# Attention columns through TensorE and ten of 24 counts through ScalarE, in the first stage of a GAT + SAGE kernel

## The reference

```python
h = relu(layernorm(x))
xp = (h @ W).reshape(N, 4, 256)                    # GAT, H = 4 heads of C = 256
a_src = einsum('nhc,hc->nh', xp, att_src);  a_dst = einsum('nhc,hc->nh', xp, att_dst)
e = leaky_relu(a_src[src] + a_dst[dst], 0.2)       # edges and self loops
alpha = softmax of e over the edges of each destination
x = x + relu(segment_sum(xp[src] * alpha, dst).reshape(N, D) + bias)
h = relu(layernorm(x))                             # then two SAGE layers
x = x + sage(relu(sage(h, W_self0, W_neigh0, b0)), W_self1, W_neigh1, b1)
```

## Time and profile before

| | us |
|---|---|
| median of 3 runs (3427.87 to 3436.28) | 3431.57 |
| profiled execution | 3438.69 |
| its span | 3437.0 |
| end of prepare's last operation (DVE L484), from the span's start | 97.77 |

### The profile page before, as it was taken

One profiled execution on the slowest core, in us unless ns is written; L12 is line 12 of the kernel. 1 busy time (PEld: TensorE's weight loads), 2 busy tenths in 40 slices (PEclk: granted clock), 3 DMA queues, 4 the chain that ended last, 5 costly groups with the idle time before them and its releaser, 6 DMA issues. The chain is left out here.

```text
span 3437.0 us, 66696 instructions
## 1 busy us (share of the span) xinstructions
PE 2969.7 (86%) x20462; PEld 1710.6 (50%) x20462; DVE 2364.8 (69%) x3944; ACT 1205.7 (35%) x2639; POOL 1637.3 (48%) x1592
## 2 busy tenths in 40 slices
PE   0558888579999997899799999998699999997998
PEld 0335554368888886444344444444344444443444
DVE  8657898599999998788566666665455555554433
ACT  3653344268888886444112222222000000001111
POOL 5002232357777775232366666663466666662000
PEclk9989998889999999899899999999899999999999
DMA  2558997369888888777699999996899999996454
GB/s 79 163 174 297 317 366 262 119 227 323 311 310 298 308 316 271 245 218 226 220 359 339 329 341 329 327 338 228 308 342 324 332 318 338 315 327 242 135 140 119
DMA packets 282530, 934.91 MB, mean 272 GB/s; under 512 B 53795, under 2 KB 54799, under 8 KB 282368
## 3 DMA queue, kind: packets, MB, share of 16 engines
q0 software_dynamic: 217792, 713.64, 59.4%
q1 hardware_dynamic: 64576, 219.26, 20.4%
HBM read 879.78 MB, written 130.57 MB: 294 GB/s over the span
## 5 line engine op out<-in xcount | busy, mean ns | idle before, releaser
L1517 PE MATMUL gagg_sum_ps<-gagg_got,gagg_hot_hi 128*128 128x256 f16 x3520 | 591.6, 273 | 94.7 <-ACT gagg_hot_hi L1488 33.0
L1405 POOL DMA_INDIRECT gagg_got<-xs_rows,all_idx x440 | 505.8, 1150 | 191.8 <-issue 132.3
L1488 ACT ACTIVATE gagg_hot_hi<-gagg_hot,all_mem 128x128 f16<-128x128 f16 x1760 | 538.0, 388 | 167.5 <-DVE gagg_hot L1428 167.5
L1405 POOL DMA_INDIRECT agg_got<-h_rows,all_idx x440 | 435.3, 989 | 320.4 <-PE agg_sum_ps L1533 182.1
L1833 POOL DMA_INDIRECT agg_got<-h_rows,all_idx x440 | 437.2, 994 | 268.1 <-PE agg_sum_ps L1986 144.5
L1453 DVE TENSOR_TENSOR sums_acc<-agg_sum_ps,sums_acc 125x1024 f32 x220 | 269.5, 1225 | 324.3 <-PE agg_sum_ps L1533 320.6
L1517 PE MATMUL gagg_sum_ps<-gagg_got,gagg_hot_lo 128*128 128x256 f16 x1760 | 481.4, 273 | 0.0
L1898 DVE TENSOR_TENSOR sums_acc<-agg_sum_ps,sums_acc 125x1024 f32 x220 | 268.8, 1222 | 247.6 <-PE agg_sum_ps L1986 245.9
L1986 PE MATMUL agg_sum_ps<-agg_got,all_mem 128*128 128x512 f16 x1760 | 414.3, 383 | 25.1 <-DVE all_mem L1867 16.7
L1533 PE MATMUL agg_sum_ps<-agg_got,agg_hot 128*128 128x512 f16 x1760 | 417.6, 380 | 20.3 <-DMA agg_got<-h_rows,all_idx 16.1
L1517 PEld LDWEIGHTS gagg_sum_ps<-gagg_got,gagg_hot_hi 128*128 128x128 f16 x3520 | 329.3, 98 | 138.3 <-ACT gagg_hot_hi L1488 70.6
(11 more groups left out here) (290 smaller groups left out, 3995.8 us busy)
## 6 DMA issues: line engine op xcount, KB each, us to landing
edg_piece<-slot_rows POOLq DMA_DIRECT2D x56, 512.0 KB
edg_w_buf<-in_L_gnn_W_self_dram SPq DMA_DIRECT2D x32, 512.0 KB, 7.8
edg_w_buf<-in_L_gnn_W_neigh_dram SPq DMA_DIRECT2D x32, 512.0 KB, 10.1
split_w<-edg_w_out SPq DMA_DIRECT2D x32, 512.0 KB, 8.9
agg_got<-h_rows,all_idx POOLq DMA_INDIRECT x880, 7.2
x_rows<-fin_val POOLq DMA_DIRECT2D x25, 500.0 KB
h_rows<-fin_h POOLq DMA_DIRECT2D x25, 500.0 KB
out_dram<-neigh_rows POOLq DMA_DIRECT2D x25, 500.0 KB
```

The lines of the kernel that those rows point to most:

```text
L1405: g.indirect_dma_start(out=got[:, k % R, :], out_offset=None, in_=rows_in[:, :], in_offset=bass.IndirectOffsetOnAxis(ap=idx[:, k:k + 1], a ...
L1488: last = a.activation(hot_hi[:, u % HOTS, h, :], hot[:, u % HOTS, :], ACT.Copy, scale=high_e[:, ds(s, 1), h])
L1517: t.matmul(sum_ps[n % 2][:, h * C:(h + 1) * C], hot_k[:, u % HOTS, h, :], got[:, u % R, part * D + h * C:part * D + (h + 1) * C], start=(u ...
```

## The change

All edits are in prepare.

- ACT makes ten of the 24 counts (borders 1 to 10) as the sum of sign(dst - t*125 + 0.5) over the row of 512 edges. POOL makes the ten offsets `lines` at the start. DVE makes the other fourteen and turns ACT's sums into counts with one small operation.
- att is loaded as 16 rows of 128 (no broadcast), and TensorE turns it into `att_c`, 128 x 16.
- For every strip k TensorE turns W's eight 128 x 128 blocks (`turn_w`, two PSUM banks of four blocks), ACT copies each bank to SBUF (`w_c`), and TensorE multiplies each block with the two att columns that belong to it (`weigh`), float32, adding up two blocks for a head in PSUM.
- POOL's weigh and ACT's gather are gone, and so is DVE's own strip (L468 to L475).
- DVE copies `w_att` out of PSUM after its four rows, then takes largest(1), then copies idx, rel and src_tile, and makes the low parts of W after these; before, the low parts came first.
- TensorE's list now holds the eight turn_w and eight weigh between the tile transposes and the transposes of the gathered rows.

```diff
-    for t in range(1, NT):
+    for t in range(BY_SIGN + 1, NT):                       # vector; BY_SIGN = 10
         last = v.tensor_scalar(junk[:, :, :], dst_f[:, :, :], float(t * TN), 0.0,
                                ALU.is_lt, ALU.add, accum_out=below[:, t - 1:t])
-        if t < NT - 1:
-            step(last)
-    last.then_inc(counted, 1)
+        step(last)
+    v.wait_ge(signed, BY_SIGN)
+    v.tensor_scalar(below[:, 0:BY_SIGN], signs[:, :], -0.5, 0.5 * CPP * CH, ALU.mult, ALU.add).then_inc(counted, 1)
...
     row(3)
+    v.wait_ge(w_att_done, KT)
+    for q in range(2):
+        last = v.tensor_copy(w_att[:, :, q * H:(q + 1) * H], w_att_ps[:, :, :, q])
+    step(last)
+    largest(1, w_att[:, :, :].rearrange("p k n -> p (k n)"))
+    v.wait_ge(turned, 1)
+    (the three copies of L478)
     for k in range(KT):
         v.wait_ge(hi_done, k + 1)
         v.scalar_tensor_tensor(w16[:, k, D:2 * D], ...)
-    (the eight products of L471, the three copies of L478)
-    v.wait_ge(tmp_used, 2 * OWN)
-    largest(1, w_att[:, :, :].rearrange("p k n -> p (k n)"))
     scale(1)
```

```diff
 @block.gpsimd
+    step(g.iota(lines[:, :], [[-TN, BY_SIGN]], base=-TN, channel_multiplier=0, ...))
+    g.tensor_scalar(lines[:, :], lines[:, :], 0.5, None, ALU.add).then_inc(lines_ready, 1)
     g.wait_ge(padded, 1)
...
-    g.dma_start(att_sb[:, q, :], att.rearrange("h c -> (h c)").partition_broadcast(P)).then_inc(att_loaded, 16)
+    g.dma_start(att_rows[q * KT:(q + 1) * KT, :], att.rearrange("h (j c) -> (h j) c", c=P)).then_inc(att_loaded, 16)
...
-    weigh(0) ... weigh(6)
```

```diff
 @block.scalar
+    a.wait_ge(lines_ready, 1)
+    a.wait_ge(dst_loaded, 32)
+    a.wait_ge(dst_tail, 16 * TAILS)
+    for t in range(BY_SIGN):
+        a.activation(junk_a[:, t], edges[:, :, 1, :], ACT.Sign, bias=lines[:, t:t + 1],
+                     accum_out=signs[:, t:t + 1]).then_inc(signed, 1)
+    a.wait_ge(att_turned, 1)
+    a.activation(att_c[:, :], att_c_ps, ACT.Copy).then_inc(att_moved, 1)
+    for n in range(KT * KT // PER_BANK):                   # 16 moves of 128 x 512
+        k, half = divmod(n, KT // PER_BANK)
+        a.wait_ge(w_turned, n + 1)
+        if k >= 2:
+            a.wait_ge(w_att_done, k - 1)
+        a.activation(w_c[:, k % 2, half * PER_BANK:(half + 1) * PER_BANK, :], w_c_ps[n % 2][:, :, :], ACT.Copy).then_inc(w_moved, 1)
     a.wait_ge(up_ready, 1)
     (the eight high parts of L366)
-    for k in range(2, OWN):
-        gather(k)
```

```diff
 @block.tensor
+    def turn_w(k):
+        for half in range(KT // PER_BANK):
+            n = k * (KT // PER_BANK) + half
+            if n >= 2:
+                t.wait_ge(w_moved, n - 1)
+            for c in range(PER_BANK):
+                j = half * PER_BANK + c
+                last = t.transpose(w_c_ps[n % 2][:, c, :], w_sb[:, k, j * P:(j + 1) * P], ident[:, :])
+            last.then_inc(w_turned, 1)
+    def weigh(k):
+        t.wait_ge(w_moved, (k + 1) * (KT // PER_BANK))
+        for j in range(KT):
+            h, first = divmod(j, KT // H)
+            last = t.matmul(w_att_ps[:, k, h, :], w_c[:, k % 2, j, :], att_of[:, j, :],
+                            start=(first == 0), stop=(first == KT // H - 1))
+        last.then_inc(w_att_done, 1)
+    t.wait_ge(made, 1)
+    t.wait_ge(att_loaded, 32)
+    t.transpose(att_c_ps, att_rows[:, :], ident[0:2 * KT, 0:2 * KT]).then_inc(att_turned, 1)
     t.wait_ge(counted, 1)
     t.matmul(start_ps[:, 0:NT - 1], ones[0:EP, :], below[:, :], start=True, stop=True).then_inc(summed, 1)
-    t.wait_ge(made, 1)
+    t.wait_ge(w_loaded, 16)
+    t.wait_ge(att_moved, 1)
+    turn_w(0)
     t.wait_ge(tiles_ready, 1)
     (the two tile transposes of L494)
+    for k in range(1, KT):
+        turn_w(k)
+        weigh(k - 1)
+    weigh(KT - 1)
     (the twelve transposes of L499 to L501)
```

More of the change, by code:

```diff
@@ L210, in prepare @@
                 EVEN = whole // 16 * 16
-                RING = 6
-                OWN = KT - 1
+                BY_SIGN = 10
+                PER_BANK = HALF // P
                 edges = sb("edges", [EP, CPP, 2, CH], i32)
@@ L247, in prepare @@
                 w_sb = sb("w_sb", [P, KT, D])
-                att_sb = sb("att_sb", [P, 2, D])
-                tmp = sb("tmp", [P, RING, D])
-                own = sb("own", [P, 2 * H, C])
+                att_rows = sb("att_rows", [2 * KT, P])
+                att_c = sb("att_c", [P, 2 * KT])
+                w_c = sb("w_c", [P, 2, KT, P])
+                lines = sb("lines", [EP, BY_SIGN])
+                signs = sb("signs", [EP, BY_SIGN])
+                junk_a = sb("junk_a", [EP, BY_SIGN, CPP, CH])
                 part_max = sb("part_max", [P, 2])
@@ L258, in prepare @@
                 src_t_ps = ps("src_t_ps", [P, HALF])
+                w_c_ps = [ps(f"w_c_ps{b}", [P, PER_BANK, P]) for b in range(2)]
+                att_ps = ps("att_ps", [P, HALF])
+                w_att_ps = att_ps[:, 0:KT * 2 * H].rearrange("p (k h q) -> p k h q", k=KT, h=H)
+                att_c_ps = att_ps[:, KT * 2 * H:KT * 2 * H + 2 * KT]
                 padded, dst_loaded, src_loaded, stored = sem("padded"), sem("dst_loaded"), sem("src_loaded"), sem("stored")
@@ L265, in prepare @@
                 fetched = [sem(f"fetched{b}") for b in range(SB)]
-                att_loaded, w_loaded, tmp_ready, tmp_used = sem("att_loaded"), sem("w_loaded"), sem("tmp_ready"), sem("tmp_used")
+                att_loaded, w_loaded, att_turned, att_moved = sem("att_loaded"), sem("w_loaded"), sem("att_turned"), sem("att_moved")
+                w_turned, w_moved, w_att_done, lines_ready, signed = sem("w_turned"), sem("w_moved"), sem("w_att_done"), sem("lines_ready"), sem("signed")
                 max_ready, reduced, up_ready, hi_done = sem("max_ready"), sem("reduced"), sem("up_ready"), sem("hi_done")
@@ L294, in _ @@
                     step = chain(g, g_step)
+                    step(g.iota(lines[:, :], [[-TN, BY_SIGN]], base=-TN, channel_multiplier=0,
+                                allow_small_or_imprecise_dtypes=True))
+                    g.tensor_scalar(lines[:, :], lines[:, :], 0.5, None, ALU.add).then_inc(lines_ready, 1)
                     g.wait_ge(padded, 1)
@@ L325, in _ @@
                     g.tensor_copy(ident_b[:, :], ident[:, :]).then_inc(made, 1)
[L327 to L331, removed]
                     def reduce(n):
@@ L336, in reduce @@
                                                bass.bass_isa.ReduceOp.max).then_inc(reduced, 1)
-                    g.wait_ge(att_loaded, 32)
-                    g.wait_ge(w_loaded, 16)
-                    weigh(0)
                     g.wait_ge(chunks_ready, 1)
@@ L346, in _ @@
                             in_offset=bass.IndirectOffsetOnAxis(ap=chunk_i[:, b:b + 1], axis=0)).then_inc(fetched[b], 16)
-                    weigh(1)
                     reduce(0)
-                    for k in range(2, OWN):
-                        weigh(k)
                     reduce(1)
@@ L463, in _ @@
                     row(3)
+                    v.wait_ge(w_att_done, KT)
[4 more added lines that the diff above has]
+                    v.wait_ge(turned, 1)
+                    for all_, ps_ in ((idx, src_ps), (rel, rel_ps), (src_tile, src_t_ps)):
+                        v.tensor_copy(all_[:, :].rearrange("p (s b) -> p s b", b=SB),
+                                      ps_[:, 0:NS].rearrange("p (b s) -> p s b", b=SB))
                     for k in range(KT):
@@ L488, in _ @@
                 def _(t):
+                    att_of = att_c[:, :].rearrange("p (q j) -> p j q", q=2)
+                    def turn_w(k):
[17 more added lines that the diff above has]
+                    t.transpose(att_c_ps, att_rows[:, :], ident[0:2 * KT, 0:2 * KT]).then_inc(att_turned, 1)
                     t.wait_ge(counted, 1)
                     t.matmul(start_ps[:, 0:NT - 1], ones[0:EP, :], below[:, :], start=True, stop=True).then_inc(summed, 1)
-                    t.wait_ge(made, 1)
+                    t.wait_ge(w_loaded, 16)
+                    t.wait_ge(att_moved, 1)
+                    turn_w(0)
                     t.wait_ge(tiles_ready, 1)
```

## The result

The changed kernel takes 3420.82 us (median of 5 runs, 3415.7 to 3423.2) against 3436.12 us (5 runs) for the kernel before; the ratio is 0.9949, 95% interval [0.9933, 0.9965]. By the ratio that is 17.5 us faster (12 to 23); the two medians differ by 15.3. It is a clear gain, but less than the 26.3 us of the sum, and the time lies outside the stated range of 3393 to 3413. From the predicted 3405 to 3420.8 there are 15.8 us. About 4.6 are the yardstick: with two more runs the median of before is that much higher than the one the prediction started from. The remaining 5 or so appear behind prepare in the profile and are not explained.

A forecast was written before the change was run, and what follows sets the result against it. POOL's strip products were taken to bound prepare's end at 97.77 us. Earlier plan, TensorE's new work and what follows put it at 71.5, saving 26.3 us: 3431.6 - 26.3 = 3405.3, forecast 3405 us, range 3393 to 3413.

The forecast's parts named there:

- the sum: Prepare's steps added up: its last operation at 71.5 us instead of 97.77, 26.3 us saved.
- The pass: TensorE's weigh in prepare: 128 float32 passes at 0.16 us, between 0.10 and 0.22, 20.5 us in all.
- The likeliest case: The sum with 0.10 to 0.22 us a pass: 3397 to 3413 us, chance 0.76.
- the case's dear end: Weigh at 0.22 us a pass: TensorE ends 7.7 us later, time 3413 us.
- Microseconds taken from it are microseconds of the kernel: Prepare's last operation at 97.77 us: the next stage begins only when all engines have met, so savings count fully.
- Rival A: TensorE rises to 2.4 GHz during the strips, DVE sets prepare's end at 60.7 us, 37 us saved; chance 0.2.
- Rival B: TensorE's passes don't overlap, 0.40 us each: kernel 4 us slower, 14 if transposes did the same; chance 0.02.
- Rival C: ACT or W late, high parts pacing DVE's low parts, two more us at most; chance 0.02 including something unseen later.
- The free terms: Prepare: ACT's signs end by 13.5 us (2.6 us cover), POOL's offsets fit its idle time, earlier W gains zero.
- The stall of 1.75 us: L422 in the plan takes 1.93 us inside POOL's strip products; with POOL idle there, 1.75 us are saved.
- The bound of the kernel before: POOL's strip products at 3.4 us each bound prepare's end, followed by ACT's sum, DVE's reduction and POOL's reduction.

The follow-up runs named there:

- wide_copies: Changed kernel with 64 moving columns (56 of them zeros) in each weigh product and the copies of idx, rel and src_tile on ScalarE; ratio 0.9907 to the kernel before.
- half_columns: Changed kernel with weigh's products loading only 64 of 128 stationary columns, the other attention columns zero; one run, prepare ends at 66.3 us, no ratio given.
- low_first: Changed kernel with W's low parts before VectorE's wait, high parts between ScalarE's moves, scale(1) before the three copies; ratio 0.9917 to the kernel before.
- counts_alone: Kernel before with only ten of the counts moved to ScalarE and the offsets on POOL; ratio 0.9988 to the kernel before.
- spin: Changed kernel with 60 idle-work products (128 x 256, float16) put where TensorE waits before the strips; ratio 0.9936 to the kernel before.

## Why the prediction was wrong, by its own steps

**The pass** is the step that failed, by its size. The sum had 128 passes at 0.16 us; they take 0.204 to 0.209, which alone is 6 us (128 x 0.045 = 5.8), the whole difference between 71.5 and 77.25. The upper bound, 0.22 from L490, was right almost to the digit; the lower, 0.10, was not a bound. It came from weight loads of transposes (80 ns for 1 column, 183 for 128) and was used for a product. The same view of the kernel before had L490's weight loads, which were a warning:

```profile
L490 PEld LDWEIGHTS tab_start_ps<-tab_below,all_ones x2: 288/313/338, 23.4 to 23.6; 100*128 100x128 f32 x2
```

313 ns for the product's load against 183 for a transpose's with the same 128 columns. Such a record is longer than the cost (333 ns in the changed kernel, where passes come every 0.204 to 0.209 us), but the distances say the same: two transposes with 128 stationary columns start 0.19 us apart, less than the passes of a product with 128 at this clock. And 24 moving columns against two was no reason to go below L490's distance, as 64 moving columns at the same level cost nothing (wide_copies). The Trainium skill ("TensorE: Matmul & The Clock Gate", LDWEIGHTS), cited in the prediction, has 107 ns for 128 columns. With it the miss would have been larger: half_columns shows 0.109 us for 64 columns of float32 at this clock.

**The likeliest case and the range.** The pass alone doesn't put the time outside: 5.8 us more on the sum are 3411, inside the range, and the saving in prepare of the case's dear end, 26.3 - 7.7 = 18.6 us, is 1.9 us from the 20.5 measured. What took it outside came on top. The range ended at this case's dear end in absolute time, with nothing for the median of three runs, which rose by 4.6, and nothing for the later stages. "Microseconds taken from it are microseconds of the kernel" is the second step that failed, as far as the profiles go: the profiled execution lost 4.9 of its 20.5 us behind prepare. Why is open.

**Rival A** was judged rightly for this kernel: TensorE stayed at 1.2 GHz for 39 us of unbroken work. The conclusion from the earlier trace rows, that transposes and narrow products don't raise the clock, came true, but those rows could not carry it: they have 2.65 us of such work (119.42 to 122.07), and wide_copies still ran at 1.2 GHz after 5 us of strips and rose all the same. In that much it was luck. The rule of the Trainium skill ("TensorE: Matmul & The Clock Gate", Part 1) that sustained matmul activity releases the clock would, read by itself, have had it rise here. Work without a gap did not raise it in this kernel, and the same work with 64 moving columns did. The price of the rival, an end at 60.7, was met within 0.1 us once the columns were wide.

**Rival B** did not happen. **Rival C** neither, in its first half: VectorE never waited for ScalarE's high parts, and low_first shows that the order behind the new wait, which the prediction took as given, was worth 10.6 us. Its second half, something unseen in later stages, had a chance of 0.02 with C and may be what the 4.9 us are.

**The free terms** were free. POOL's offsets are ready at 1.79 us, before its first load could go at 2.07. W came at 18.96 instead of 21.64 and TensorE still waited 2.58 us for the tile numbers. ScalarE's signs ended at 14.25 rather than 13.5, since its table load stood behind the wait for dst; DVE's fourteenth count ended at 16.45, so 2.2 us of cover were left. The stall of 1.75 us went, and counts_alone shows that it went with POOL's products and not with the counts.

**The bound of the kernel before** was POOL, but not as told. The prediction let the end pass through ScalarE's last sum and DVE's reduction, and took POOL's products at 3.4 us each. Four lines of the kernel before and one of the changed kernel (the last) tell it otherwise. In the views of a single line, "a/b/c" are the shortest, median and longest duration in ns, followed by the first and last start in us; POOLq is POOL's queue.

```profile
L331 POOL TENSOR_TENSOR tab_tmp<-tab_w_sb,tab_att_sb x14: 2332/2516/11897, 21.6 to 87.9; 128x1024 f32<-128x1024 f32 x14
L335 POOLq MODIFY_POOL_CONFIG  x4: 1/14/28, 42.7 to 90.5; - x4
L331 POOLq MODIFY_POOL_CONFIG  x2: 83/83/83, 48.7 to 48.7; - x2
96.07 0.38 POOL L335 PARTITION_ALL_REDUCE tab_all_max<-tab_part_max  x1 [5.79 <-issue]
L340 POOLq MODIFY_POOL_CONFIG  x2: 32/32/32, 29.7 to 29.7; - x2
```

In the kernel before, each time POOL goes from products to its reduction over partitions or back, a MODIFY_POOL_CONFIG is issued, and the next operation starts much later: 42.7 to 48.36 and 90.5 to 96.07 for the two reductions, 48.7 to 56.36 for the product between them. These three changeovers leave POOL idle for 5.57, 7.63 and 5.79 us, 19 us of its chain. So the end was set by POOL's last product and the changeover: DVE's request came at 92.45 and POOL started 3.6 us after it, while ScalarE and DVE were beside the path. The first of the ten late products takes 11.9 us instead of about 2.5; it runs beside VectorE's low parts (56.08 to 65.65) and ends at 68.3. The changed kernel has no products on POOL and one changeover, at 29.7, while DVE takes the big maximum; its second reduction starts 0.1 us after the request (63.20 to 63.30) and takes 0.35 us, where the prediction had 4.1 for both.

## What to carry to other kernels

Price an operation by a row of the same operation, not by its neighbour in form: with 128 stationary columns two transposes came 0.19 us apart and two passes of a float32 product 0.204 to 0.209, and the one row of the right kind, L490, was nearly exact at 0.22. When a wait is put on an engine, list what that engine could do in the meantime: the order behind the new wait was worth half as much in prepare as the change itself. And where passes with 128 stationary columns and hardly any moving ones fill TensorE, try more moving columns: 64 instead of two cost nothing here and brought the clock with them. Beyond 64 nothing was tried. Last, look at what an engine does between its operations: 19 us of POOL's chain were changeovers between two kinds of work.

## What the runs showed of the hardware that was not expected

- A float32 product with two moving columns costs 0.204 to 0.209 us a pass with 128 stationary columns and 0.109 with 64, both at 1.2 GHz; at 2.4 GHz 128 columns cost 0.109 with 64 moving columns and 0.106 with two (spin, 24.60 to 26.30 for sixteen). Two moving columns or 64 make no difference at either level (0.206 with 64 at 1.2 GHz, wide_copies).
- TensorE stayed at 1.2 GHz through 39 us without a gap (transposes and two-column products) and fell from 2.4 GHz to it amid such work; with 64 moving columns, even zeros, it rose within the first strip in two runs and within the second in the third (wide_copies: a busy time of 3.51 us for the first strip's passes, 2.67 for the second's, 1.90 from then on). The windows of the profile print a clock of 1.00 for the changed kernel's strips all the same:

```profile
30.00:35.00 5.00, 5.00 (x26) 5.00 (x25) 5.00 (x1) 1.18 (x3) 0.00 (x0) 1.00 0.07 23
```

  The clock is to be read from durations there: transposes 0.217 us apart are the level of 1.2 GHz. In spin the same window prints 0.50, after the engine has once been up.
- A changeover of POOL between elementwise products and its reduction over partitions (MODIFY_POOL_CONFIG on its queue) takes 5.5 to 5.6 us before the reduction and 7.1 to 7.7 us before the next product, in both profiles of the kernel before and in counts_alone. Without one the reduction starts 0.1 us after its request.
- Two small VectorE operations of 0.26 us took 2.28 and 2.40 us beside POOL's products of 128 x 1024.
